# The first head's loads issued behind the last stores of the first stage, on two queues, and the bound's stores issued by ScalarE

## The chip, the cores and the metric

The kernel runs on one core of one Trainium2 chip. The metric is device time in microseconds of one execution. A core has TensorE (PE, matmuls), VectorE (DVE), ScalarE (ACT), GpSimd (POOL) and SyncE (SP), which run side by side and wait for each other on semaphores, and 16 DMA engines, to which SyncE and ScalarE both issue transfers through queues of their own.

## What is computed

A transformer block on x of shape (4, 2048, 256), in float32: a layer norm, then attention with 16 heads of width 16 and an FFN with weights of plus and minus one, both on the normalised x, and both added to x.

```python
xn = _layernorm(x)
# attention: b=4, n=2048, d=256, H=16, Dh=16
q = _rope(split(xn @ Wq + bq)); k = _rope(split(xn @ Wk + bk)); v = split(xn @ Wv + bv)
scores = jnp.einsum('bhnd,bhmd->bhnm', q, k) / jnp.sqrt(jnp.float32(d))
inter = jnp.einsum('bhnm,bhmd->bhnd', jax.nn.softmax(scores, axis=-1), v)
attn = inter.transpose(0, 2, 1, 3).reshape(b, n, d) @ Wo + bo
# FFN: connection weights k0 (512x1024), k1 (1024x1024), k2 (1024x256) are booleans, read as +1 / -1
h = s0 * conn(k0, concat([xn, -xn])); h = relu(h) * 2
h = s1 * conn(k1, h); h = relu(h) * 2
h = s2 * conn(k2, h)
return x + attn + h
```

## The kernel before

The program has three blocks, one behind the other, each ended by a barrier of all engines. `prepare` is the first stage, `maxima` is left at once on these inputs (a branch on a flag, `loose`), and `attend` takes nearly all of the time.

**prepare** works through the 8192 tokens in NC = 16 chunks of 512, numbered c. For a chunk, ScalarE issues the load of x and normalises it, TensorE turns it (`turn`) and projects it to queries, keys and values, VectorE multiplies by the rotary tables (`products`), GpSimd adds the two products (`turned`, L557) and subtracts the high part (`parts`, L550), and ScalarE makes the square and the high part (`part`, L399 and L402). SyncE stores, each 512 KB: the normalised chunk (`store_x`, L298), four pieces of queries and keys split into high and low parts (`store_parts`, L305; in the trace q_parts and k_parts, two calls each), and the values (L340). All of these go to DRAM. The buffer `parts` has four places, so L402 of one piece waits until the store of the piece four before has landed. In SyncE's program a chunk runs: two stores of key parts (of the chunk before), the normalised chunk c + 1, two stores of query parts, the values. The order is written out by hand in the loop behind `store_x(0)`.

Into this loop other transfers are put by hand. `load_first(c)` issues at c = 5 the loads of two biases, at FIRST_HEAD_AT = 13 two tiny DMAs that write a row of zeros into `q_rows` (`row_of_bound`, L311) and the first half of what attend needs for its first head, at c = 14 the second half and the load of the first 512 tokens (`xT_lo`, L321). Half a head is five DMAs in `load_rows` (L806 to L810): keys 256 KB, keys again 128 KB, and three loads of queries of 64 KB. The data are those of the first batch, stored in chunks 0 to 3. In DRAM the parts are an array of [4, 64 x 8, 2048], so the 32 rows that the first DMA writes come from a view with an outer dimension of 4 (4 x 8 rows), and the 16 rows of each of the others from a view with an outer dimension of 2 (2 x 8 rows). Rows are 8 KB for keys and 4 KB for queries.

Behind chunk 15 a bound on all scores is worked out by a chain over several engines (`keep_norms`, `bound_scores`, the square root on ScalarE at L454, `spread_bound`). VectorE fills `bound_fill` with it and SyncE writes it into the first head's rows (`row_of_bound`, L311) and, for the other heads, into DRAM (`store_shift`, four DMAs of 128 KB, L276). SyncE then waits at L351 to L359 until all loads and stores of the stage but those of `store_shift` have landed, and the block ends. VectorE in the meantime splits `xT_lo` (L702, L704), which waits for its load.

**attend** runs 16 passes of four heads. TensorE's first matmuls of scores (L1029) use head 0, which prepare has loaded. SyncE first waits for `bound_stored`, which counts the landed DMAs of `store_shift`, and then loads head 1 with `load_rows`, now all twelve DMAs (L806 to L812; the last of each half is the bound's row, 8 KB), the values of head 1 and the residual. A head is loaded when the one two before it is done with its scores.

```python
            sp.wait_ge(first_loaded, 16 * (LOADS - 2))
            sp.wait_ge(fill_stored, FILLS)
            sp.wait_ge(bound_row, 32)
```

Of the kernel before, what the change touches and what calls it, by code (L numbers as in the profile page):

```python
# [22 lines left out]
F32 = mybir.dt.float32  # L23
# [5 lines left out]
P = 128  # L29
B, N, D, H = 4, 2048, 256, 16  # L30
DH = D // H
T = B * N
G = B * H
# [8 lines left out]
PARTS = 2  # L42
# [5 lines left out]
FIRST_HEAD_AT = 13  # L48
# [88 lines left out]
def prepare(nc, a, w, scratch, bound_stored):  # L137

    ctx = ExitStack()
    with ctx:  # L140
# [126 lines left out]

        def here(c):
            return slice((c % CB) * C, (c % CB + 1) * C)

        @block.sync
        def _(sp):
            def store_shift(a, filled, landed):
                to = scratch["shift"][a].rearrange("g (h w n) -> w (g h) n", h=P // G, n=FILL)
                for n in range(G * N // (P * FILL)):
                    sp.dma_start(to[n], filled.bitcast(F32)).then_inc(landed, 16)  # L276

# [15 lines left out]
            store_shift(1, fill[:], fill_stored)  # L293
# [64 lines left out]
        def _(act):  # L358
# [93 lines left out]
            part(4 * NC - 1)  # L452
# [885 lines left out]
```

## Time and profile before

| | |
|---|---|
| time, median of 3 runs | 2648.11 us (2647.49 to 2648.26) |
| the profiled execution: its own time | 2645.93 us |
| the profiled execution: its span | 2644.1 us |
| TensorE busy | 2577.4 us, 97% of the span |
| ScalarE busy | 2099.3 us, 79% |
| VectorE busy | 977.5 us, 37% |
| GpSimd busy | 300.0 us, 11% |
| first stage (prepare) | from 0 to about 240 us |
| mean granted clock of TensorE | 0.989 of full speed |

The span runs from the first instruction to the last of the profiled execution; its own time has some 2 us more around it. Busy time is the time in which an engine computes; issuing a DMA or waiting does not count. In the view by stretches a row gives, for a piece of the span, the busy time of each engine in us with the number of instructions in brackets (PE, PEld for weight loads, DVE, ACT, POOL), the clock granted to TensorE as a part of full speed, the mean busy share of the 16 DMA engines (packets that overlap on one engine can bring it above 1), and what they moved in GB/s.

### The profile page before, as it was taken

The numbers are of one execution on the slowest core, as the hardware profiler recorded it, in microseconds if no ns is written. First come the engines' busy times: TensorE is split into PE (matmuls) and PEld (weight loads), VectorE is DVE, ScalarE is ACT, GpSimd is POOL, SyncE is SP. The second block draws the span as 40 slices with busy tenths as digits, with TensorE's granted clock in tenths as the row PEclk, the third lists the DMA queues.
The fourth block names the chain that finished last, engine by engine and source line by source line (L and its number), as shares of the span: only waits on it lengthen the run. The fifth ranks groups of instructions, "written<-read, shape, count | busy, mean of one in ns | idle before, by whom it ended". The sixth has DMA issues, their size and how long they took to land.

```text
span 2644.1 us, 49178 instructions
## 1 busy us (share of the span) xinstructions
PE 2577.4 (97%) x20711; PEld 1340.4 (51%) x20711; DVE 977.5 (37%) x1665; ACT 2099.3 (79%) x2342; POOL 300.0 (11%) x268
## 2 busy tenths in 40 slices
PE   7886999999999999999999999999999999999999
PEld 5663454444445454545445454544445454544545
DVE  7773323343324233243324233243324233242323
ACT  6885888888888878788887878788887878788884
POOL 6783000000000000000000000000000000000000
PEclk9997999999999999999999999999999999999999
DMA  9995111111212112121212212121212212121212
GB/s 283 294 292 171 37 47 52 53 61 49 57 43 75 51 48 71 50 77 53 78 44 70 63 46 70 53 77 51 77 43 67 61 53 69 57 77 49 77 38 97
DMA packets 202199, 210.45 MB, mean 80 GB/s; under 512 B 144685, under 2 KB 148605, under 8 KB 195577
## 3 DMA queue, kind: packets, MB, share of 16 engines
q1 hardware_dynamic: 199672, 198.91, 25.1%
q10 hardware_dynamic: 2304, 8.39, 0.9%
q8 instruction: 163, 2.67, 0.4%
q14 instruction: 60, 0.48, 0.1%
HBM read 131.34 MB, written 75.89 MB: 78 GB/s over the span
## 4 chain that ended last, share of the span: by engine, by line
PE 91%; ACT 0%; DVE 0%; issue 0%; DVEq 0%; SPq 0%
PE ps_o L1042 37%; PE ps_f L1075 27%; PE ps_s L1029 24%; PE ps_y L1088 2%; PE ps_s L1124 0%; PE ps_f L1124 0%; ACT probs L1009 0%; DVE probs L1266 0%; PE ps_f L1132 0%; PE ps_o L1124 0%; PE ps_y L1124 0%; PE ps_s L1132 0%; DVEq L819 0%; PE ps_o L1132 0%; PE ps_y L1132 0%
## 5 line engine op out<-in xcount | busy, mean ns | idle before, releaser
L1009 ACT ACTIVATE probs<-ps_s 128x1024 f32<-128x1024 f32 x2048 | 1930.0, 1034 | 453.1 <-PE ps_s L1029 450.7
L1042 PE MATMUL ps_o<-probs,v_ones 128*32 128x512 f32 x8192 | 1011.3, 600 | 0.0
L1029 PE MATMUL ps_s<-q_rows,k_rows 50*128 50x512 f32 x4096 | 868.9, 439 | 5.1 <-SPq L981 4.1
L1029 PEld LDWEIGHTS ps_s<-q_rows,k_rows 50*128 50x128 f32 x4096 | 365.7, 184 | 672.2 <-ACT probs L1009 600.3
L1042 PEld LDWEIGHTS ps_o<-probs,v_ones 128*32 128x32 f32 x8192 | 200.6, 108 | 418.3 <-issue 295.8
L1075 PE MATMUL ps_f<-h_hi,ffn_w 64*128 64x512 f32 x2048 | 410.2, 393 | 0.0
L1075 PE MATMUL ps_f<-h_lo,ffn_w 64*128 64x512 f32 x2048 | 409.3, 391 | 0.0
L1209 DVE COPY raw<-ps_f 128x512 f32<-128x512 f32 x256 | 164.9, 686 | 560.4 <-PE ps_f L1075 560.4
L1164 POOL TENSOR_TENSOR heads<-heads,sums 128x512 f32<-128x512 f32 x64 | 82.3, 1285 | 2149.8 <-DVE sums L1185 2149.8
L1185 DVE RECIPROCAL sums<-sums 128x128 f32<-128x128 f32 x256 | 226.6, 924 | 1.7
L1075 PEld LDWEIGHTS ps_f<-h_lo,ffn_w 64*128 64x128 f32 x2048 | 198.7, 186 | 34.2
L1075 PEld LDWEIGHTS ps_f<-h_hi,ffn_w 64*128 64x128 f32 x2048 | 197.7, 186 | 23.9
L1176 DVE COPY heads<-ps_o 128x512 f32<-128x512 f32 x64 | 44.3, 692 | 407.8 <-PE ps_o L1042 407.8
L1220 DVE SCALAR_TENSOR_TENSOR h_lo<-raw,h_hi 128x512 fp32r<-128x512 f32 x256 | 177.3, 693 | 8.7
L1075 PE MATMUL ps_f<-ffn_w,h_hi 64*128 64x256 f32 x1024 | 129.0, 277 | 0.0
L1075 PE MATMUL ps_f<-ffn_w,h_lo 64*128 64x256 f32 x1024 | 128.5, 276 | 0.0
L1203 DVE SCALAR_TENSOR_TENSOR rest_sum<-ps_f,ffn_scale,rest_sum 128x512 f32<-128x512 f32 x32 | 22.6, 746 | 246.4 <-PE ps_f L1075 246.4
L1075 PE MATMUL ps_f<-xT_hi,ffn_w 64*128 64x512 f32 x512 | 109.0, 421 | 0.0
L1218 DVE TENSOR_SCALAR h_hi<-raw 128x512 fp32r<-128x512 f32 x256 | 107.3, 419 | 0.0
L1075 PE MATMUL ps_f<-xT_lo,ffn_w 64*128 64x512 f32 x512 | 102.4, 395 | 0.0
L1075 PEld LDWEIGHTS ps_f<-ffn_w,h_lo 64*128 64x128 f32 x1024 | 97.5, 185 | 5.5
L1075 PEld LDWEIGHTS ps_f<-ffn_w,h_hi 64*128 64x128 f32 x1024 | 97.5, 185 | 2.6
(118 smaller groups left out, 1384.6 us busy)
## 6 DMA issues: line engine op xcount, KB each, us to landing
k_rows<-k_parts SPq DMA_DIRECT2D x128, 256.0 KB
q_rows<-q_parts SPq DMA_DIRECT2D x384, 64.0 KB
q_parts<-parts SPq DMA_DIRECT2D x32, 512.0 KB, 8.7
k_parts<-parts SPq DMA_DIRECT2D x32, 512.0 KB, 8.3
k_rows<-k_parts SPq DMA_DIRECT2D x128, 128.0 KB
x_chunk<-in_x ACTq DMA_DIRECT2D x16, 512.0 KB, 7.3
xn_d<-xn_t SPq DMA_DIRECT2D x16, 512.0 KB, 8.6
v_heads<-v_sb SPq DMA_DIRECT2D x16, 512.0 KB, 7.7
```

Of the source, the lines that this page charges most:

```text
L1009: nc.scalar.activation(probs[:, s % PBUF, half * 2 * C:(half + 1) * 2 * C], ps_s[:, half].rearrange("p c n -> p (c n)"), ACT.Exp, scale=SC ...
L1029: last = nc.tensor.matmul(ps_s[:, half, w], k_rows[rows, u, t * P:(t + 1) * P], q_rows[rows, u, half], start=True, stop=True)
L1042: last = nc.tensor.matmul(ps_o[32 * c:32 * c + 2 * DH], v_ones[:, u, t], probs[:, s % PBUF, c * C:(c + 1) * C], start=(t == 0), stop=(t == ...
L1075: last = nc.tensor.matmul(to, lhs, rhs, start=first and stage == 0, stop=final and stage == 1)
L1088: last = nc.tensor.matmul(ps_y[:, n], headsT[:, k, t * P:(t + 1) * P], wo[:, k], start=(k == 0), stop=(k == DT - 1))
L1164: nc.gpsimd.tensor_tensor(heads[:, u], heads[:, u], sums[:, u], ALU.mult).then_inc(heads_ready, 1)
L1176: nc.vector.tensor_copy(heads[:, u], ps_o[:]).then_inc(raw_ready, 1)
L1185: nc.vector.reciprocal(at, at).then_inc(sums_inverted, 1)
L1203: nc.vector.scalar_tensor_tensor(out=to, in0=ps_f[:, bank], scalar=w["scale"][:, 0:1], in1=to, op0=ALU.mult, op1=ALU.add).then_inc(group_u ...
L1209: nc.vector.tensor_copy(raw[:, bank], ps_f[:, bank]).then_inc(group_used, 1)
L1218: nc.vector.tensor_scalar(hi, raw[:, bank], 0.0, None, ALU.max).then_inc(high_ready, 1)
L1220: nc.vector.scalar_tensor_tensor(out=lo, in0=raw[:, bank], scalar=0.0, in1=hi.bitcast(F32), op0=ALU.max, op1=ALU.subtract).then_inc(part_r ...
```

## The change

- The loads of the first head leave chunks 13 and 14. All of them, with the load of `xT_lo`, are issued behind the last two stores of parts: `xT_lo` and the four loads of keys by SyncE (`load_first_keys`), the six loads of queries by ScalarE (`load_queries`), ahead of its square root for the bound.
- The four stores of the bound (`store_shift`) are issued by ScalarE, behind the square root and a table load for Exp, when the bound is filled in. SyncE keeps the two small `row_of_bound`.
- The loads of `bv` and `bo` move from chunk 5 to chunk 4, the two rows of zeros from chunk 13 to chunk 4, all behind the load of `Wo` (`load_constants`).
- `load_rows` is cut into `load_keys`, `load_queries` and `load_shift`. In attend a head is still loaded by the same twelve DMAs, now all keys first, then all queries, then the bound's rows.
- SyncE still waits for all ten loads of the first head at the end of prepare.

```diff
-            def load_first(c):
-                if c == FIRST_HEAD_AT:
-                    sp.wait_ge(k_rows_set, 1)
-                    for w_half in range(2):
-                        row_of_bound(1, fill[:], w_half, zero_row)
-                if FIRST_HEAD_AT <= c < FIRST_HEAD_AT + 2:
-                    load_rows(sp, scratch, 0, w["q_rows"][:, 0], w["k_rows"][:, 0], first_loaded, only=c - FIRST_HEAD_AT)
-                if c == FIRST_HEAD_AT + 1:
-                    sp.dma_start(w["xT_lo"][:].bitcast(F32).rearrange("p k n -> p (k n)"), scratch["xn"][0]).then_inc(first_x_loaded, 16)
-                if c == FFN_WEIGHTS_AT + 1:
-                    sp.dma_start(bv[:], a["bv"].rearrange("(k p) -> p k", p=P), allow_slow_non_contiguous=True).then_inc(bias_loaded, 16)
-                    sp.dma_start(bo[:], a["bo"].rearrange("(o n) -> o n", o=1).broadcast_to([P, D])).then_inc(bias_loaded, 16)
+            def load_constants():
+                sp.wait_ge(w_split, 1)
+                sp.dma_start(w["wo"][:], a["Wo"].rearrange("(k p) n -> p k n", p=P)).then_inc(wo_loaded, 16)
+                sp.dma_start(bv[:], a["bv"].rearrange("(k p) -> p k", p=P), allow_slow_non_contiguous=True).then_inc(bias_loaded, 16)
+                sp.dma_start(bo[:], a["bo"].rearrange("(o n) -> o n", o=1).broadcast_to([P, D])).then_inc(bias_loaded, 16)
+                for w_half in range(2):
+                    row_of_bound(1, fill[:], w_half, zero_row)
+
+            def load_first_keys():
+                sp.dma_start(w["xT_lo"][:].bitcast(F32).rearrange("p k n -> p (k n)"), scratch["xn"][0]).then_inc(first_x_loaded, 16)
+                sp.wait_ge(k_rows_set, 1)
+                load_keys(sp, scratch, 0, w["k_rows"][:, 0], first_loaded)
 
             store_x(0)
             for c in range(NC):
-                load_first(c)
                 if c == FFN_WEIGHTS_AT:
-                    sp.wait_ge(w_split, 1)
-                    sp.dma_start(w["wo"][:], a["Wo"].rearrange("(k p) n -> p k n", p=P)).then_inc(wo_loaded, 16)
+                    load_constants()
...
             store_parts(4 * NC - 2)
             store_parts(4 * NC - 1)
+            load_first_keys()
             sp.wait_ge(fill_ready, 2)
             for w_half in range(2):
                 row_of_bound(0, bound_fill, w_half, bound_row)
-            store_shift(0, bound_fill, bound_stored)
-
             sp.wait_ge(first_loaded, 16 * (LOADS - 2))
...
             part(4 * NC - 1)
+            load_queries(act, scratch, 0, w["q_rows"][:, 0], first_loaded)
             act.wait_ge(bound2_ready, 1)
             nc.scalar.activation(bound[:], bound2[:], ACT.Sqrt).then_inc(bound_ready, 1)
             nc.scalar.activation(std[:, 0, 0:1], eps[:], ACT.Exp)
+            act.wait_ge(fill_ready, 2)
+            store_shift(act, 0, bound_fill, bound_stored)
...
+def load_keys(queue, scratch, g, k_rows, loaded):
+
+    k_head, q_head = heads_of(scratch)
+    for w in range(2):
+        at = GROUP_ROWS * w
+        queue.dma_start(k_rows[at:at + 2 * DH, :].bitcast(F32), k_head[g]).then_inc(loaded, 16)
+        queue.dma_start(k_rows[at + 2 * DH:at + AUG, :].bitcast(F32), k_head[g, 0:2]).then_inc(loaded, 16)
+
+
+def load_queries(queue, scratch, g, q_rows, loaded):
+
+    k_head, q_head = heads_of(scratch)
     q_flat = q_rows.rearrange("p h n -> p (h n)")
     for w in range(2):
         at = GROUP_ROWS * w
         here = slice(w * N // 2, (w + 1) * N // 2)
...
+        queue.dma_start(q_flat[at:at + DH].bitcast(F32), q_head[g, 0:2, :, here]).then_inc(loaded, 16)
+        queue.dma_start(q_flat[at + DH:at + 2 * DH].bitcast(F32), q_head[g, 0:2, :, here]).then_inc(loaded, 16)
+        queue.dma_start(q_flat[at + 2 * DH:at + AUG].bitcast(F32), q_head[g, 2:4, :, here]).then_inc(loaded, 16)
```

SyncE's queue from the values of chunk 12 to the last stores of key parts, before (128x... are the stores of a chunk, 32x, 16x the loads of a head):

```order
L340 DMA v_heads<-v_sb 128x1024
L311 DMA q_rows<-fill 1x4x256 x2
L806 DMA k_rows<-k_parts 32x1x2048
L807 DMA k_rows<-k_parts 16x1x2048
L808 DMA q_rows<-q_parts 16x1x1024
L809 DMA q_rows<-q_parts 16x1x1024
L810 DMA q_rows<-q_parts 16x1x1024
L305 DMA k_parts<-parts 128x2x512 x2
L298 DMA xn_d<-xn_t 128x1024
L305 DMA q_parts<-parts 128x2x512 x2
```

The same again, with the load of `xT_lo` at its end, stands behind the values of chunk 13. After the change the stores of chunks 12 to 15 follow each other with nothing between them, and the keys stand behind the last pair; the end of SyncE's queue in prepare is now:

```order
L304 DMA q_parts<-parts 128x2x512 x2
L337 DMA v_heads<-v_sb 128x1024
L304 DMA k_parts<-parts 128x2x512 x2
L321 DMA xT_lo<-xn_d 128x1024
L801 DMA k_rows<-k_parts 32x1x2048
L802 DMA k_rows<-k_parts 16x1x2048
L801 DMA k_rows<-k_parts 32x1x2048
L802 DMA k_rows<-k_parts 16x1x2048
L310 DMA q_rows<-q_rows 1x4x256 x2
```

Here the four stores of row_shift, which stood behind L311 before, are gone. On ScalarE the end of prepare is, after the change (before, the activations and the table load stood alone):

```order
L812 DMA q_rows<-q_parts 16x1x1024
L813 DMA q_rows<-q_parts 16x1x1024
L814 DMA q_rows<-q_parts 16x1x1024
L812 DMA q_rows<-q_parts 16x1x1024
L813 DMA q_rows<-q_parts 16x1x1024
L814 DMA q_rows<-q_parts 16x1x1024
L451 ACTIVATE bound<-bound 1x1
L452 ACT_TABLE_LOAD
L452 ACTIVATE std<-eps 128x1
L270 DMA row_shift<-q_rows 128x256 x4
```

So six loads of queries come ahead of the square root, and the stores of the bound have moved behind it from SyncE's queue.

## Rows read from the trace of the kernel before

**Rows 1.** the page: busy time and instructions of TensorE; the chain that ended last

```profile
PE 2577.4 (97%) x20711; PEld 1340.4 (51%) x20711; DVE 977.5 (37%) x1665; ACT 2099.3 (79%) x2342; POOL 300.0 (11%) x268
...
PE 91%; ACT 0%; DVE 0%; issue 0%; DVEq 0%; SPq 0%
```

**Rows 2.** chain of waits in order of time, start us, us, what: where attend begins

```profile
240.83 0.81 PE ps_s L1029 x2
```

**Rows 3.** timeline of SyncE's queue, chunks 12 to attend: start us, us, line, DMA

```profile
173.82 2.87 SPq L305 DMA_DIRECT2D k_parts<-parts  x2
...
183.34 2.05 SPq L311 DMA_DIRECT2D q_rows<-fill  x2
185.43 0.70 SPq L806 DMA_DIRECT2D k_rows<-k_parts  x1
...
189.04 1.08 SPq L305 DMA_DIRECT2D k_parts<-parts  x2
...
202.39 2.84 SPq L305 DMA_DIRECT2D k_parts<-parts  x2
...
219.90 2.85 SPq L305 DMA_DIRECT2D k_parts<-parts  x2
...
229.72 1.67 SPq L305 DMA_DIRECT2D k_parts<-parts  x2
234.33 1.29 SPq L311 DMA_DIRECT2D q_rows<-q_rows  x2
235.66 1.90 SPq L276 DMA_DIRECT2D row_shift<-q_rows  x4
240.70 0.76 SPq L806 DMA_DIRECT2D k_rows<-k_parts  x1
```

**Rows 4.** timeline of ScalarE: its two long waits in chunks 13 to 15

```profile
200.39 0.63 ACT L402 ACTIVATE parts<-turned 128x512 fp32r<-128x512 f32 x1 [6.76 <-DMA k_parts<-parts]
...
217.91 0.63 ACT L402 ACTIVATE parts<-turned 128x512 fp32r<-128x512 f32 x1 [8.71 <-DMA k_parts<-parts]
```

**Rows 5.** stretches: busy time by engine (instructions), clock, DMA share, GB/s; first stage

```profile
162.33:173.82 11.49, 10.56 (x61) 8.27 (x61) 9.13 (x21) 11.00 (x20) 10.12 (x9) 1.00 1.05 326
187.00:190.00 3.00, 1.36 (x11) 1.36 (x12) 1.86 (x3) 3.00 (x6) 3.00 (x3) 1.00 0.30 92
...
217.00:220.00 3.00, 0.00 (x0) 0.00 (x0) 0.00 (x0) 2.00 (x4) 1.39 (x2) 0.84 0.15 60
```

**Rows 6.** stretches in attend: head 1 loading, then no load, then head 2 loading

```profile
244.00:249.00 5.00, 4.79 (x22) 3.31 (x22) 0.00 (x0) 3.63 (x5) 0.00 (x0) 0.50 0.24 92
...
254.00:258.00 4.00, 4.00 (x37) 2.06 (x34) 1.55 (x3) 4.00 (x5) 0.00 (x0) 1.00 0.12 51
269.00:278.00 9.00, 9.00 (x76) 4.05 (x70) 2.58 (x5) 6.90 (x8) 0.00 (x0) 1.00 0.00 0
...
293.00:297.00 4.00, 4.00 (x34) 2.02 (x36) 3.91 (x7) 2.96 (x4) 0.00 (x0) 1.00 0.13 52
```

**Rows 7.** a stretch: chunk 15, from its first store of keys to the last

```profile
219.90:229.72 9.82, 4.44 (x20) 2.91 (x20) 3.40 (x5) 5.47 (x10) 9.79 (x8) 0.50 0.70 227
```

**Rows 8.** timeline of SyncE's queue, the load of Wo in chunk 4

```profile
69.53 0.75 SPq L331 DMA_DIRECT2D wo<-in_Wo  x1
71.33 3.08 SPq L305 DMA_DIRECT2D k_parts<-parts  x2
```

**Rows 9.** stretches behind the last stores of parts

```profile
229.70:235.50 5.80, 2.27 (x9) 1.30 (x6) 3.82 (x12) 1.69 (x3) 3.00 (x2) 0.50 1.05 260
235.70:238.20 2.50, 1.06 (x3) 0.34 (x1) 1.15 (x2) 0.00 (x0) 0.00 (x0) 0.50 0.72 210
```

**Rows 10.** SyncE's waits at the end of the first stage

```profile
L355 SPq EVENT_SEMAPHORE  x4: 28/28/333, 237.7 to 238.2; - x4
```

**Rows 11.** timelines of ScalarE and VectorE in the tail

```profile
232.88 0.20 ACT L454 ACTIVATE bound<-bound 1x1 f32<-1x1 f32 x1 [3.23 <-DVE bound L631]
...
235.20 1.23 DVE L704 TENSOR_TENSOR xT_lo<-xT_lo,xT_hi 128x1024 fp32r<-128x1024 f32 x1
```

More of the change, by code:

```diff
@@ L47 @@
 FFN_WEIGHTS_AT = 4
-FIRST_HEAD_AT = 13
 FILL = 256
@@ L266, in prepare, with store_shift @@
         block = ctx.enter_context(nc.Block())
+        def store_shift(queue, a, filled, landed):
+            to = scratch["shift"][a].rearrange("g (h w n) -> w (g h) n", h=P // G, n=FILL)
+            for n in range(G * N // (P * FILL)):
+                queue.dma_start(to[n], filled.bitcast(F32)).then_inc(landed, 16)
         def here(c):
@@ L272, in _ @@
         def _(sp):
[L273 to L276, printed above, removed]
             sp.dma_start(ident[:], a["ident"]).then_inc(ident_loaded, 16)
@@ L292, in _ @@
             sp.wait_ge(zero_ready, 1)
-            store_shift(1, fill[:], fill_stored)
+            store_shift(sp, 1, fill[:], fill_stored)
             def store_x(c):
@@ L794, in heads_of @@
     return (scratch[name].rearrange("am (g e) n -> g am e n", e=HALF) for name in ("k", "q"))
-def load_rows(sp, scratch, g, q_rows, k_rows, loaded, only=None):
+def load_keys(queue, scratch, g, k_rows, loaded):
     k_head, q_head = heads_of(scratch)
-    shift = scratch["shift"].rearrange("a g (w n) -> g w a n", w=2)
+    for w in range(2):
[4 more added lines that the diff above has]
+    k_head, q_head = heads_of(scratch)
     q_flat = q_rows.rearrange("p h n -> p (h n)")
@@ L804, in load_rows, with load_shift @@
         here = slice(w * N // 2, (w + 1) * N // 2)
-        if only in (None, w):
-            sp.dma_start(k_rows[at:at + 2 * DH, :].bitcast(F32), k_head[g]).then_inc(loaded, 16)
-            sp.dma_start(k_rows[at + 2 * DH:at + AUG, :].bitcast(F32), k_head[g, 0:2]).then_inc(loaded, 16)
-            sp.dma_start(q_flat[at:at + DH].bitcast(F32), q_head[g, 0:2, :, here]).then_inc(loaded, 16)
-            sp.dma_start(q_flat[at + DH:at + 2 * DH].bitcast(F32), q_head[g, 0:2, :, here]).then_inc(loaded, 16)
-            sp.dma_start(q_flat[at + 2 * DH:at + AUG].bitcast(F32), q_head[g, 2:4, :, here]).then_inc(loaded, 16)
-        if only is None:
-            sp.dma_start(q_flat[at + AUG:at + ROWS].bitcast(F32), shift[g, w]).then_inc(loaded, 16)
+        queue.dma_start(q_flat[at:at + DH].bitcast(F32), q_head[g, 0:2, :, here]).then_inc(loaded, 16)
+        queue.dma_start(q_flat[at + DH:at + 2 * DH].bitcast(F32), q_head[g, 0:2, :, here]).then_inc(loaded, 16)
+        queue.dma_start(q_flat[at + 2 * DH:at + AUG].bitcast(F32), q_head[g, 2:4, :, here]).then_inc(loaded, 16)
+def load_shift(queue, scratch, g, q_rows, loaded):
+    shift = scratch["shift"].rearrange("a g (w n) -> g w a n", w=2)
+    q_flat = q_rows.rearrange("p h n -> p (h n)")
+    for w in range(2):
+        at = GROUP_ROWS * w + AUG
+        queue.dma_start(q_flat[at:at + PARTS].bitcast(F32), shift[g, w]).then_inc(loaded, 16)
 def attend(nc, a, w, scratch, out, bound_stored):
@@ L895, in load_head @@
             def load_head(g, u):
-                load_rows(sp, scratch, g, q_rows[:, u], k_rows[:, u], rows_loaded[u])
+                load_keys(sp, scratch, g, k_rows[:, u], rows_loaded[u])
+                load_queries(sp, scratch, g, q_rows[:, u], rows_loaded[u])
+                load_shift(sp, scratch, g, q_rows[:, u], rows_loaded[u])
             def load_v(g, u):
```

## The prediction

> **What bounds the kernel now.** The page comes first: TensorE is busy for 97% of the span and holds 91% of the chain that ended last [rows 1]. That is attend, and attend keeps its instructions. So the change can only move the moment at which attend begins, plus whatever its own loads do there. The chain in order of time dates that moment: the first matmul of scores is at 240.83 [rows 2]. Every microsecond by which this comes earlier or later is one in the total.
>
> Next, SyncE's timeline [rows 3], read for the pace of the chunks. Two stores of keys are issued at the start of each. An undisturbed chunk takes 11.49 us from one such issue to the next [rows 5]. From 173.82 on the distances are 15.22, 13.35, 17.51 and 9.82 us. The first three are long, and what stands between them are the two halves of the first head's loads. ScalarE's timeline shows how it hurts: L402 waits 6.76 and 8.71 us for the landing of a store of parts [rows 4].
>
> Third, why a few loads cost so much. The stretches say it. In the undisturbed chunk the DMA engines have a share of 1.05 and move 326 GB/s. From 187 to 190 and from 217 to 220 the share is 0.30 and 0.15, 92 and 60 GB/s [rows 5], while everyone waits for a DMA. A share of 0.15 is 2.4 of 16 engines. So most engines have run empty, and some two still work off a backlog.
>
> Attend shows the same loads without other traffic. With no head on the way the share is 0.00. While head 1 (issued from 240.70 on [rows 3]) and head 2 come in, it is 0.24, that is 4 engines, and then 0.12 and 0.13 at 51 and 52 GB/s, that is **two engines at 25.5 to 26 GB/s each** [rows 6]. I read it with the code: the view with outer dimension 4 goes over four engines, those with outer dimension 2 over two. Of 1152 KB, engines 0 and 1 (my names for the two) then carry per half 256/4 + 128/2 + 3 x 64/2 = 224 KB, in all 448 KB each, or 459 thousand bytes. At 25.5 GB/s that is **18.0 us**, although the whole, spread evenly, would be 72 KB per engine. The rows agree with it: head 1 is issued from 240.70 on, and at 254 to 258 the two engines are still busy.
>
> **Step 1: chunks 13 to 15 without the loads.** Chunk 12 starts its key stores at 173.82. Chunks 12 and 13 then take the undisturbed 11.49 us each. Chunk 14 loads no x any more (3.0 MB in place of 3.5), so it lies between the undisturbed pace, 11.49, and that of GpSimd, which has eight operations per chunk and is busy 9.79 of 9.82 us in chunk 15 [rows 7]; I take 10.3, nearer to GpSimd's, since 11.49 x 3.0/3.5 is 9.85. Chunk 15 stays at GpSimd's 9.82. The last stores of keys are then issued at 173.82 + 2 x 11.49 + 10.3 + 9.82 = 216.9, in place of 229.72: **-12.8 us** (-11.6 with 11.49 for chunk 14, -13.3 with 9.82). The issue of the loads (from 185.43 to 189.04 for the first half) goes with them and is part of the distances.
>
> **Step 2: the end of the stage.** Call the issue of the last key stores T (229.72 before, 216.9 now). Before, SyncE passed its last wait at 238.2 [rows 10], T + 8.5. Its waits were nearly all over by then: what set the end was the chain of the bound, two small DMAs and 1.90 us for four stores of row_shift [rows 3]. Now, behind T, engines 0 and 1 have to do in turn:
> - the stores that are under way or just issued: until T + 5.8, the stretch with a share of 1.05 in the rows of before [rows 9];
> - `xT_lo`, 512 KB over 16 engines, 33 thousand bytes each at 25.5: 1.3 us;
> - the loads of the first head: 18.0 us;
> - the stores of row_shift, 512 KB at 210 GB/s in the stretch in which they ran before [rows 9]: 2.5 us, of which I count 1.6, since ScalarE's queue shares the engine with SyncE's and small packets leave room.
>
> Sum T + 26.7, with a half microsecond for the last landing and the wait T + 27.2, that is 244.1 in place of 238.2. So step 2 costs **+18.7 us**. That the loads come from two queues changes nothing in it: the engines are the bottleneck, not the issue. Two queues save issue time only, at most 10 x 0.70 us, and this lies far inside the 27 us.
>
> The bounds. Below: engines 0 and 1 take the stores of the tail faster, since the total is what limited them there (260 GB/s is 16 per engine), by the bytes: values, two stores, `xT_lo`, row_shift are 5 x 33 thousand at 25.5, 6.4 us, with 18.0 and a start of 1.5 gives T + 25.9. Above: while stores run, the engine gives 326/16 = 20.4 GB/s; all 459 thousand bytes at that are 22.5 us, T + 31.7.
>
> The Trainium skill (DMA: Bandwidth & Descriptors, Specifications) states about 27 GiB/s per engine. By that, as an estimate, 459 thousand bytes would take 15.8 us, and the change would cost 2.2 us less than in my sum. The rows show 25.5 to 26, so they decide here.
>
> **Step 3: what is hidden.** ScalarE issues six loads (0.70 us each as SyncE's [rows 3], 4.2) ahead of its square root, which was due at T + 3.2 [rows 11]; the bound comes some 1.0 us later, then SyncE's two small DMAs. All that is done by T + 9, hidden by the loads; with that cover gone it would cost 1.0. VectorE's split of `xT_lo` ran to 236.4 [rows 11]; now it waits for the landing, T + 8 to T + 13, plus 1.23 us and two shorter instructions: hidden, too. SyncE saves the 1.90 us of row_shift, which count for nothing behind the loads. Attend's SyncE waits for `bound_stored` before head 1; those stores are in front of the last keys or level with them, and head 1 has a whole head's time to come in (the two-engine stretches of heads 1 and 2 lie 39 us apart [rows 6]), so nothing waits. The other order of the twelve DMAs in attend is free for that reason. TensorE's clock is at its lower level, 1.2 GHz, at attend's start already (0.50 in the stretch from 244 to 249 [rows 6]), so a longer wait ahead of it has nothing more to take.
>
> **Step 4: the constants.** In chunk 4 SyncE now issues two biases (as Wo, 0.75 each) and two rows of zeros (2.05 [rows 3]) ahead of the key stores at 71.33 [rows 8]. Without them Wo ended 1.05 us before that, so the store goes out some 2.5 us late. The DMA engines have a backlog there as everywhere in these chunks (share 1.05), so its landing moves little: 0, at most +2. In chunk 13 the rows of zeros fell into free time (183.34 to 185.39), so taking them away brings nothing.
>
> **Sum:** -12.8 + 18.7 + 0 = **+5.9 us**. Against the profiled execution's 2645.93 that is 2651.8; this execution lies 2.2 below the median of the runs, 2648.11, so for the median 2654.0. About 0.2% (5.3 us) is what a measurement of this kernel can tell from no change, so the forecast stands just beyond it. Its own range, from the bounds: -13.3 + 17.4 = +4.1 to -11.6 + 23.2 + 1 = +12.6; the upper end needs everything to go wrong together, so 2651.5 to 2658.5.
>
> **Rivals.**
> - *The two queues work on different engines.* No row shows narrow loads from ScalarE, whose only DMAs are the wide loads of x. If its six went to another pair of engines, the keys alone would be 256 KB on SyncE's pair, 10.3 us, and the end T + 5.8 + 1.3 + 10.3 + 1 = T + 18.4, 235.3: -2.9 us, 2645.2, no change that can be told. In attend all loads come from one queue and share one pair, which says nothing on this. The Trainium skill (the same page, "Why a DMA increments its semaphore by 16 and not by 1") says that such a DMA takes the lowest-numbered engines whichever of the two queues it is on, and no run here shows it yet.
> - *The loads hide in the tail (the other side).* If the two-engine plateau were attend's own, and the loads ran wide, 1.7 MB at 326 GB/s are 5.2 us behind T + 5.8, the end T + 11.5 at 228.4: -9.8, 2638.3. It decides at T + 21.3: a load stage that ends before that makes the kernel faster. Against it: in chunks 13 to 15 the same few engines were seen at work [rows 5].
> - *The chunks gain less.* If chunk 14 and 15 find another wait, so that each keeps some 1.9 us of the length that it had, step 1 is worth -9, and the time is 2657.8. For it: chunk 14 of before took 17.51 us, and that the loads made all of this is read off, not shown.
> - *A small loss.* Step 1 is right, but the two engines catch up in the tail more than I grant: +2 to +5, 2650 to 2653.
>
> **How the numbers follow.** Forecast 0.55, queues on different engines 0.10, hidden 0.07, less gain 0.10, small loss 0.18. Slower by over 0.2% (above 2653.4): 0.45 of the forecast's 0.55 and the less gain, 0.55. Within 0.2%: the rest of the forecast, the small loss, most of the different engines: 0.36. Faster: 0.09. The range takes the forecast, the small loss and less gain, and reaches down to half of the first rival: 2646.5 to 2659.
>
> **What would show it.** Right: issues of key stores every 11.5 us up to chunk 14, the last near 217; the waits of L402 on key stores gone; then a stretch of some 15 us with a share of 0.12 to 0.25 at 50 to 100 GB/s, SyncE waiting at the end of prepare for `q_rows` or `k_rows`, and TensorE's first scores near 247. Wrong: a share of 0.25 to the end with 4 engines busy (first rival), or first scores before 240.8.

## The result and the profile after

The changed kernel takes 2653.26 us (median of 20 runs, 2651.21 to 2655.72), the kernel before 2647.60 us in the same series (20 runs, 2645.21 to 2650.29). The ratio is 1.0022 with a 95% interval of 1.0015 to 1.0029: **slower by 5.7 us**, where +5.9 was forecast. The profiled execution of the changed kernel took 2651.77 us with a span of 2650.0, the one of before 2645.93 and 2644.1. Of the runs below, one of the eleven executions of e1 was slow (4905.28 us) and has no part in its ratio.

SyncE's timeline of the changed kernel, from chunk 12 to attend (start us, us, line, DMA):

```profile
173.40 2.85 SPq L304 DMA_DIRECT2D k_parts<-parts  x2
...
184.76 2.86 SPq L304 DMA_DIRECT2D k_parts<-parts  x2
...
194.92 2.88 SPq L304 DMA_DIRECT2D k_parts<-parts  x2
...
205.77 2.97 SPq L304 DMA_DIRECT2D k_parts<-parts  x2
...
216.82 1.66 SPq L304 DMA_DIRECT2D k_parts<-parts  x2
218.52 1.11 SPq L321 DMA_DIRECT2D xT_lo<-xn_d  x1
219.68 0.73 SPq L801 DMA_DIRECT2D k_rows<-k_parts  x1
...
222.48 1.27 SPq L310 DMA_DIRECT2D q_rows<-q_rows  x2
247.33 0.75 SPq L801 DMA_DIRECT2D k_rows<-k_parts  x1
```

The key stores now go out at distances of 11.36, 10.16, 10.85 and 11.05 us, where they were 15.22, 13.35, 17.51 and 9.82 [rows 3]. The last are issued at 216.82 in place of 229.72: 12.9 us have been won in the chunks. Then SyncE issues its loads at once, 0.73 us for a load of keys, and is done with everything at 223.75. But its first DMA in attend is issued at 247.33, where it was 240.70.

ScalarE's six loads do not stand strictly behind the last stores. ScalarE does not wait for SyncE, and its first load goes out 1.2 us ahead of T, the issue of the last key stores (216.82). Its timeline:

```profile
215.60 1.23 ACTq L812 DMA_DIRECT2D q_rows<-q_parts  x1
```

What SyncE did in between is in the view of its own waits (engine line, waited for: us in total, times, longest us), and in the line of that wait:

```profile
SPq L351 <- DMA q_rows<-q_rows: 20.8, 1, 20.8
```

```profile
L351 SPq EVENT_SEMAPHORE  x4: 28/28/18867, 223.9 to 244.8; - x4
```

L351 is the wait for the first head's loads, 20.8 us, over at 244.8. Before, the line that answers to it was passed at 238.2 with next to no wait [rows 10]. The view by stretches of the changed kernel shows for what it waited (busy time by engine, clock, DMA share, GB/s):

```profile
187.00:190.00 3.00, 2.97 (x20) 2.27 (x21) 3.00 (x5) 3.00 (x7) 3.00 (x4) 1.00 1.00 193
205.77:216.82 11.05, 3.63 (x24) 2.10 (x22) 3.40 (x5) 6.21 (x11) 9.90 (x8) 0.88 0.91 274
216.80:222.60 5.80, 1.47 (x7) 0.57 (x3) 2.92 (x10) 1.69 (x3) 3.00 (x2) 0.50 1.05 226
220.00:224.00 4.00, 1.87 (x5) 1.64 (x6) 0.89 (x5) 1.69 (x3) 0.00 (x0) 0.50 1.09 177
228.00:234.00 6.00, 0.00 (x0) 0.00 (x0) 2.25 (x3) 0.00 (x0) 0.00 (x0) 0.50 0.29 111
234.00:244.00 10.00, 0.00 (x0) 0.00 (x0) 0.00 (x0) 0.00 (x0) 0.00 (x0) 0.50 0.13 51
```

The hole of before at 187 to 190 [rows 5] is filled: share 1.00, 193 GB/s. In its place stands the stretch from 234 to 244: no engine computes, and the DMA share is 0.13 at 51 GB/s, as head 1 (0.12 at 51) and head 2 (0.13 at 52) had shown in attend [rows 6]. By the prediction's count these are two engines with 448 KB each, now with the whole core waiting. TensorE's first scores, with the idle time ahead of them in brackets:

```profile
247.46 1.22 PE L1042 MATMUL ps_s<-q_rows,k_rows 50*128 50x512 f32 x4 [22.70 <-SPq L994]
```

247.46 in place of 240.83 [rows 2] is 6.6 us later; the span grew by 5.9. Attend gave back 0.7 us. That fits TensorE's clock: it rises to 2.4 GHz about 7.6 us behind the first scores (at 255.1) where it took about 8.9 before (at 249.8), and 1.3 us less at half the clock are 0.65 us. The stretches of 1 us in which it rises, before and then after:

```profile
249.00:250.00 1.00, 1.00 (x10) 0.38 (x11) 0.23 (x1) 0.94 (x1) 0.00 (x0) 0.62 0.25 87
```

```profile
255.00:256.00 1.00, 1.00 (x10) 0.57 (x6) 0.09 (x1) 0.83 (x2) 0.00 (x0) 0.92 0.13 50
```

### The profile page after: what moved, and what is told of

Read it like the earlier page. It is cut to its first block, busy times and chain, and to the rows that moved or that the text cites. A ratio compares the mean times of both kernels' runs of the same rounds, so it can differ in the third digit from the quotient of the medians.

```text
span 2650.0 us, 49178 instructions
## 1 busy us (share of the span) xinstructions
PE 2572.1 (97%) x20711; PEld 1334.4 (50%) x20711; DVE 978.3 (37%) x1665; ACT 2099.1 (79%) x2342; POOL 299.9 (11%) x268
## 4 chain that ended last, share of the span: by engine, by line
PE 90%; ACT 0%; DVE 0%; issue 0%; DVEq 0%; SPq 0%
PE ps_o L1055 36%; PE ps_f L1088 27%; PE ps_s L1042 24%; PE ps_y L1101 2%; PE ps_s L1137 0%; PE ps_f L1137 0%; ACT probs L1022 0%; DVE probs L1279 0%; PE ps_f L1145 0%; PE ps_o L1137 0%; PE ps_y L1137 0%; PE ps_s L1145 0%; DVEq L830 0%; PE ps_y L1145 0%; PE ps_o L1145 0%
## 5 line engine op out<-in xcount | busy, mean ns | idle before, releaser
L1042 PE MATMUL ps_s<-q_rows,k_rows 50*128 50x512 f32 x4096 | 868.3, 439 | 23.7 <-SPq L994 22.7
```

The lines of the kernel that those rows point to most:

```text
L1042: last = nc.tensor.matmul(ps_s[:, half, w], k_rows[rows, u, t * P:(t + 1) * P], q_rows[rows, u, half], start=True, stop=True)
```

## The experiments

All of e1 to e12 are timed in five rounds against the kernel before. In this table T is the issue of the last key stores in the profiled execution, and the next column the first scores of attend; the last is the median less that of before in the same series. T and the first scores are each from one execution. Runs with the same order of stores in the chunks differ by up to 1.6 us in T (the change and e1 to e4: 215.27 to 216.82), so less than that in T is not read as an effect.

| run | median us | ratio to before (95% interval) | T | first scores | behind T | us against before |
|---|---|---|---|---|---|---|
| before | 2647.60 | 1 | 229.72 | 240.83 | 11.1 | 0 |
| the change | 2653.26 | 1.0022 (1.0015 to 1.0029) | 216.82 | 247.46 | 30.6 | +5.7 |
| e1: change, loads of 8 rows | 2641.91 | 0.9982 (0.9973 to 0.9991) | 216.08 | 236.72 | 20.6 | -4.3 |
| e2: change, queries of 8 rows | 2648.07 | 1.0005 (0.9996 to 1.0015) | 215.27 | 242.04 | 26.8 | +1.9 |
| e3: change, one queue | 2653.58 | 1.0025 (1.0016 to 1.0035) | 216.79 | 248.38 | 31.6 | +7.4 |
| e4: change, bound by SyncE | 2650.86 | 1.0017 (1.0008 to 1.0026) | 216.19 | 246.19 | 30.0 | +4.6 |
| e5: before, loads of 8 rows | 2641.91 | 0.9984 (0.9975 to 0.9993) | 224.12 | 235.40 | 11.3 | -4.3 |
| e6: change, rows together | 2627.06 | 0.9928 (0.9914 to 0.9941) | 205.36 | 222.16 | 16.8 | -19.1 |
| e7: before, rows together | 2623.43 | 0.9914 (0.9901 to 0.9928) | 208.41 | 219.15 | 10.7 | -22.7 |
| e8: e7, chunks 14 and 15 | 2624.64 | 0.9917 (0.9904 to 0.9931) | 209.09 | 219.58 | 10.5 | -21.5 |
| e9: before, bound by ScalarE | 2647.65 | 1.0003 (0.9994 to 1.0012) | 231.03 | 242.57 | 11.5 | +0.8 |
| e10: e7, 8 rows | 2627.73 | 0.9931 (0.9917 to 0.9944) | 211.81 | 222.54 | 10.7 | -19.2 |
| e11: e6, 8 rows | 2628.94 | 0.9934 (0.9920 to 0.9947) | 206.06 | 223.81 | 17.8 | -17.9 |
| e12: e6, two engines | 2720.85 | 1.0283 (1.0269 to 1.0297) | 205.55 | 239.60 | 34.1 | +74.0 |

### e1: the same bytes over more engines

```diff
-        queue.dma_start(k_rows[at:at + 2 * DH, :].bitcast(F32), k_head[g]).then_inc(loaded, 16)
-        queue.dma_start(k_rows[at + 2 * DH:at + AUG, :].bitcast(F32), k_head[g, 0:2]).then_inc(loaded, 16)
+        for m in range(4):
+            queue.dma_start(k_rows[at + HALF * m:at + HALF * (m + 1), :].bitcast(F32), k_head[g, m]).then_inc(loaded, 16)
+        for m in range(2):
+            row = at + 2 * DH + HALF * m
+            queue.dma_start(k_rows[row:row + HALF, :].bitcast(F32), k_head[g, m]).then_inc(loaded, 16)
...
+        for n, m in enumerate((0, 1, 0, 1, 2, 3)):
+            row = at + HALF * n
+            queue.dma_start(q_flat[row:row + HALF].bitcast(F32), q_head[g, m, :, here]).then_inc(loaded, 16)
```

> The changed kernel with the first head's ten loads cut into 24 of 8 rows each (one outer slice of the DRAM view per DMA), the same bytes from the same two queues in the same place. Theory (two DMA engines carry 448 KB each): with outer dimension 8 a DMA goes over 8 engines, the busiest engine carries 144 KB, 5.8 us at 25.5 GB/s in place of 18.0, so 12 us less at the end of prepare: first scores near 235 in place of 247.5, about 2641.5 us, and no stretch with a DMA share of 0.13. Rival 1 (the bytes behind the last stores cost, however spread): no change, 2653. Rival 2 (number of DMAs and their issue cost): 14 more at 0.65 us, 7 per queue, slower than the changed kernel by up to 4 us.

Measured: 2641.91, 4.3 us less than before and 10.0 less against before than the change. The first scores came at 236.72, 20.6 behind T in place of 30.6. A stretch of its profile where the changed kernel had two engines:

```profile
229.00:232.00 3.00, 0.00 (x0) 0.00 (x0) 2.25 (x3) 0.00 (x0) 0.00 (x0) 0.50 0.50 199
...
234.00:236.00 2.00, 0.00 (x0) 0.00 (x0) 0.00 (x0) 0.00 (x0) 0.00 (x0) 0.50 0.00 0
```

Share 0.50 is eight engines, at 199 GB/s 24.9 each, and from 234 on nothing is left. There are more DMAs than in the change and the same bytes in the same place, and the time fell: this is against both rivals named. The time from T to the first scores fell by 10.0, where 12.2 was expected from the two-engine sum. The loads themselves ran at the expected 25 GB/s per engine, so the missing 2 us lie elsewhere behind T; no run shows where.

### e2: half of the dose

```diff
-            load_queries(act, scratch, 0, w["q_rows"][:, 0], first_loaded)
+            first_queries(act, scratch, 0, w["q_rows"][:, 0], first_loaded)
```

(`first_queries` is the loop over six slices of e1; the keys stay as in the change.)

> The changed kernel with ScalarE's six loads of queries cut into twelve of 8 rows, SyncE's keys as they are. A half dose of the first run. Theory: the two engines keep 256 KB of keys each and get 48 KB of queries in place of 192, 304 in place of 448 KB, 144 KB less at 25.5 GB/s: 5.8 us less than the changed kernel, 2647.5, with the stretch of two engines shorter by that. Rival (the queries are not on the engines of the keys, so only the keys set the end): no change, 2653. Rival (what the 8-row cut gained came of the keys' shape alone): no change too.

Measured: 2648.07, +1.9 against before where the change has +5.7: 3.7 us less than the change, where 5.8 were expected. (That the median is so near to the expected 2647.5 is owed to a series in which before, too, took 1.4 us less.) This speaks against the first rival of the prediction as well: the queries are ScalarE's, and making them wide shortens the wait for SyncE's keys by 3.8 us (26.8 behind T in place of 30.6). So **both queues' narrow loads ran on the same two engines**.

### e3 and e4: the two other parts of the change undone

```diff
-            load_queries(act, scratch, 0, w["q_rows"][:, 0], first_loaded)
...
                 load_keys(sp, scratch, 0, w["k_rows"][:, 0], first_loaded)
+                load_queries(sp, scratch, 0, w["q_rows"][:, 0], first_loaded)
```

> The changed kernel with the six loads of queries issued by SyncE behind the keys, so that all ten come from one queue. Theory (both queues' narrow loads run on the same two engines, which are the bottleneck): the same time within 1 us, 2653; SyncE's end of issue moves by 4 us, hidden. Rival (the second queue brings other engines or more rate per engine): slower by 4 to 7 us, 2657 to 2660.

Measured: 2653.58, +7.4 against before where the change has +5.7; the intervals overlap, and the profile has the first scores 1.0 us further behind T. From 234 to 244 its profile reads like that of the change:

```profile
234.00:244.00 10.00, 0.00 (x0) 0.00 (x0) 0.00 (x0) 0.00 (x0) 0.00 (x0) 0.50 0.13 52
```

The second queue is worth 1 to 2 us at the most, and not the 4 to 7 of the rival.

```diff
             for w_half in range(2):
                 row_of_bound(0, bound_fill, w_half, bound_row)
+            store_shift(sp, 0, bound_fill, bound_stored)
...
-            act.wait_ge(fill_ready, 2)
-            store_shift(act, 0, bound_fill, bound_stored)
```

> The changed kernel with the four stores of the bound back on SyncE. Theory: hidden behind the loads, no change (within 1 us of 2653). Rival (ScalarE's issue of them is what gains or costs at the end of prepare): 1.9 us either way.

Measured: 2650.86, +4.6 against before. That is 1.0 us below the change by the differences, with intervals that overlap, and 0.6 us by the place of the first scores behind T. Nothing that five rounds can tell, and in no case 1.9 us.

### e9: the bound's stores by ScalarE, alone, without the cover

```diff
             for w_half in range(2):
                 row_of_bound(0, bound_fill, w_half, bound_row)
-            store_shift(0, bound_fill, bound_stored)
...
             nc.scalar.activation(std[:, 0, 0:1], eps[:], ACT.Exp)
+            act.wait_ge(fill_ready, 2)
+            store_shift(act, 0, bound_fill, bound_stored)
```

> The kernel before with one part of the change alone: the four stores of the bound issued by ScalarE, so nothing of the first head's loads hides it. Rival (my reading in the prediction, that SyncE's 1.90 us of issue for these stores are part of what set the end of prepare): 1.9 us less than before. Theory after a second look: the two small DMAs of the bound's row end their issue at 235.6 and land about 2 us later, and SyncE waited 0.3 us for them at 238.2 even behind the four stores, so no more than 0.5 us is to be had: the same as before.

Measured: 2647.65, ratio 1.0003: no change. The line of SyncE's last waits in this kernel (there L353) is the reason:

```profile
L353 SPq EVENT_SEMAPHORE  x4: 28/28/2707, 237.1 to 239.9; - x4
```

Without the four stores SyncE comes to its wait 1.9 us earlier, at 237.1 behind a T of 231.03, and stands there 2.7 us, until 239.9, for its two small DMAs to land. T + 8.9 in place of T + 8.5. The prediction had said that the issue of these stores was part of what set the end of prepare; it was not.

### e5: the wide loads left among the chunks

The kernel before with the same cut, in `load_first`; nothing else moves.

```diff
                 if FIRST_HEAD_AT <= c < FIRST_HEAD_AT + 2:
-                    load_rows(sp, scratch, 0, w["q_rows"][:, 0], w["k_rows"][:, 0], first_loaded, only=c - FIRST_HEAD_AT)
+                    first_half(sp, scratch, w["q_rows"][:, 0], w["k_rows"][:, 0], first_loaded, c - FIRST_HEAD_AT)
```

> The kernel before, with the first head's loads left in chunks 13 and 14 but cut into 24 DMAs of 8 rows. Theory (the chunks wait for two overloaded engines, 12.8 us for 448 KB each): with 144 KB on 8 engines the excess of chunks 12 to 14 over 11.4 us each falls to about a third, 4 us, so the last key stores go out near 221 and the time is about 2639 (8 to 9 us less than before). Rival (SyncE's issue of the loads holds up the stores behind them): 12 DMAs per half at 0.65 us are 7.8 us in place of 3.6, the stores go out later than before and the time is the same as before or up to 8 us more.

Measured: 2641.91, in the same place as e1. T fell from 229.72 to 224.12, 5.6 us, where 8 to 9 were expected. So of the 12.9 us that the narrow loads cost the chunks, 7 to 8 remain with wide ones. An estimate of what the bytes alone take there is 5.2 us: 1.7 MB at the 326 GB/s of an undisturbed chunk, in which the DMA engines are busy all the time (share 1.05 [rows 5]). SyncE's timeline shows no long hold-up by the issue: the key stores behind the first half go out at 189.39 where they went at 189.04 before. The rival is out, the size of the theory was too large.

### e6 and e7: the rows of a head together in DRAM

```diff
-        "q": dram("q_parts", [2 * PARTS, G * HALF, N], F32),
+        "q": dram("q_parts", [PARTS, G * DH, N], F32),
...
-        q_out = scratch["q"].rearrange("(a m) (b p) (r n) -> b m r p a n", m=2, p=P, n=C)
+        q_out = scratch["q"].rearrange("a (b p m) (r n) -> b m r p a n", m=2, p=P, n=C)
...
-    return (scratch[name].rearrange("am (g e) n -> g am e n", e=HALF) for name in ("k", "q"))
+    return (scratch[name].rearrange("a (g e) n -> g a e n", e=DH) for name in ("k", "q"))
...
+        for n, part in enumerate((0, 1, 0)):
+            queue.dma_start(k_rows[at + DH * n:at + DH * (n + 1), :].bitcast(F32), k_head[g, part]).then_inc(loaded, 16)
...
+        for n, part in enumerate((0, 0, 1)):
+            queue.dma_start(q_flat[at + DH * n:at + DH * (n + 1)].bitcast(F32), q_head[g, part, :, here]).then_inc(loaded, 16)
```

(The same for the keys' array. A store of parts still has 128 rows with two pieces of 2 KB, but the rows of one store now lie 16 KB apart in DRAM in place of 8 KB. In attend the heads are loaded by the new views, too.)

> The changed kernel with another order of rows in DRAM: the 16 rows of a head's high (or low) part lie together, so that each load is one slice of 16 rows (12 loads of the first head in place of 10, same bytes; the stores keep 128 rows of 2 KB pieces). Theory: 16 engines with 72 KB each, 2.9 us in place of the 5.8 of the run with 8 rows: 3 us less than that run's 2641.9, so 2639, first scores near 234. Rival (with the loads spread, something else sets the end of prepare: the bound's chain, the stores of the bound): 2641 to 2642. Rival (the new order makes the stores of parts slower, in all chunks): above 2645.

> The kernel before with the same order of rows in DRAM, loads still in chunks 13 and 14. With 448 KB on the busiest engine chunks 12 to 15 lost 13 us, with 144 KB 8 us; theory: by that slope 72 KB leave some 6.5 us, the time is 2640.5. What stays is the bytes themselves: 1.7 MB at 320 GB/s are 5.3 us in chunks that are limited by the DMA engines. Rival (only the busiest engine matters): 2 us left, 2636.

Measured: 2627.06 and 2623.43, 12 and 17 us below what was expected. The miss is not at the end but in all chunks: T is at 205.36 and 208.41. The stores themselves have become faster. From the DMA issues, the kernel before and e7 (median us from issue to landing in the last column):

```profile
q_parts<-parts SPq DMA_DIRECT2D x32, 512.0 KB, 8.7
k_parts<-parts SPq DMA_DIRECT2D x32, 512.0 KB, 8.3
```

```profile
q_parts<-parts SPq DMA_DIRECT2D x32, 512.0 KB, 4.3
k_parts<-parts SPq DMA_DIRECT2D x32, 512.0 KB, 3.2
```

From 8.7 and 8.3 us to 4.3 and 3.2. The same stretches of the first stage, before and then e7:

```profile
90.00:120.00 30.00, 25.38 (x136) 20.62 (x133) 20.72 (x48) 26.75 (x48) 22.92 (x19) 0.89 0.98 297
120.00:150.00 30.00, 24.50 (x145) 19.50 (x144) 23.28 (x47) 25.28 (x44) 23.06 (x19) 1.00 1.00 301
```

```profile
90.00:120.00 30.00, 26.77 (x155) 21.41 (x154) 23.11 (x49) 28.95 (x50) 26.42 (x22) 1.00 0.89 323
120.00:150.00 30.00, 27.82 (x159) 21.41 (x157) 24.30 (x56) 28.54 (x52) 26.24 (x22) 1.00 0.88 317
```

More bytes at a smaller share (323 GB/s at 0.89 for 297 at 0.98), so the DMA engines are no longer full, and GpSimd is busy 26.4 of 30 us in place of 22.9. This gain has nothing to do with the change under study, which stays a loss on top of it: e6 takes 3.6 us more than e7. No run here says which property of the order makes the gain.

The 2.9 us for the loads did not come true, either. Sixteen engines do not carry them eight times as fast as two. Here is e7 between 178 and 181, where the loads of the first half of the head (issued from 175.59 to 178.34) meet the next stores, against 182 to 188, stores and loads of x.

```profile
178.00:181.00 3.00, 3.00 (x21) 2.21 (x19) 3.00 (x6) 3.00 (x8) 3.00 (x3) 1.00 0.97 124
182.00:188.00 6.00, 5.90 (x36) 4.81 (x34) 2.90 (x5) 4.31 (x8) 5.24 (x5) 1.00 1.05 412
```

In attend of e6 the same loads run with next to nothing beside them (head 1, issued from 222.03 on):

```profile
225.00:228.00 3.00, 2.80 (x12) 1.90 (x14) 0.00 (x0) 2.84 (x3) 0.00 (x0) 0.50 1.04 131
```

All engines are busy at 124 and 131 GB/s, 8 GB/s per engine, where stores run at 412. So these loads wait for something that more engines don't add to; what it is, no run shows. 1.2 MB at 124 GB/s are 9.5 us and not 2.9. The loads of 8 rows in e1 do not have this limit (24.9 GB/s per engine). In e6 the first scores come 16.8 behind T, about what was expected (the 20.6 of e1 less 3), but the stores behind T have become faster as well, so this agreement says nothing for the 2.9 us.

### e8, e10, e11: what is the best place and the best cut

e8 is e7 with `FIRST_HEAD_AT = 14`. e10 and e11 are e7 and e6 with each of the 16-row loads in two of 8 rows:

```diff
-            queue.dma_start(k_rows[at + DH * n:at + DH * (n + 1), :].bitcast(F32), k_head[g, part]).then_inc(loaded, 16)
+            for e in (slice(0, HALF), slice(HALF, DH)):
+                queue.dma_start(k_rows[at + DH * n + e.start:at + DH * n + e.stop, :].bitcast(F32), k_head[g, part, e]).then_inc(loaded, 16)
```

> The run before this one (rows together, loads among the chunks) with FIRST_HEAD_AT = 14, so the halves go out at the start of chunks 14 and 15, which move 3.0 and 2.5 MB of their own in place of 3.5 and 3.0. Theory: these chunks are nearer to GpSimd's pace, 9.8 us, and have DMA time left, so 3 us less than FIRST_HEAD_AT = 13: 2637.5. Rival: the loads land late and hold up the end of prepare, or the last stores: same or 1 to 3 us more, 2641 to 2643.

> Rows together in DRAM and the loads in chunks 13 and 14 (2623.4 with 16-row loads), each load now cut into two of 8 rows, in attend too. The 16-row loads showed a share of 1.0 at only 107 to 143 GB/s, the 8-row loads of the first run 198 GB/s at a share of 0.5. Theory: what the loads cost in the chunks (3 us by the pace of the run without them) is the rate at which they run, so 1 us less, 2622.5. Rival: the number of DMAs on SyncE's queue (24 in place of 12) costs 1 to 3 us, 2625.

> Rows together and the loads behind the last stores on two queues (2627.1 with 16-row loads), each cut into two of 8 rows. Behind the last stores 1.2 MB at 130 GB/s are 9 us, at 198 GB/s 6 us. Theory: 2 to 3 us less, 2624.5, the end of prepare at T + 11. Rival (more issue at the end, 24 DMAs over two queues): same or 1 to 2 us more, 2627 to 2629.

Measured: 2624.64, 2627.73, 2628.94. All three theories missed. The later chunks give nothing (+1.2 against e7). In e10 the twelve loads of a half are on SyncE's queue ahead of the stores, which go out at 181.07 where e7 had 178.38 (0.9 of these 2.7 us are there already when the first load goes out). This fits the rival, the number of DMAs, though the time is 3.6 us above e7 by the differences and it had said 1 to 3. In e11 T is the same as in e6 within 0.7 us and the end is 1.0 further behind it, as its rival said.

### e12: two engines again, in the new order

```diff
-    return (scratch[name].rearrange("a (g e) n -> g a e n", e=DH) for name in ("k", "q"))
+    return (scratch[name].rearrange("a (g e m) n -> g a m e n", e=HALF, m=2) for name in ("k", "q"))
...
-            queue.dma_start(q_flat[at + DH * n:at + DH * (n + 1)].bitcast(F32), q_head[g, part, :, here]).then_inc(loaded, 16)
+            queue.dma_start(q_flat[at + DH * n:at + DH * (n + 1)].bitcast(F32), q_head[g, part, :, :, here]).then_inc(loaded, 16)
```

The same rows go to the same number of partitions, only the outer dimension of the view is 2 in place of 16. (Within a part the order of a head's rows changes, alike for queries and keys.)

> The run with rows together and the loads behind the last stores (2627.1), but each load reads the same 16 rows through a view with outer dimension 2, so that only the number of engines changes, not DRAM's order. This takes the two effects of that run apart. Theory: chunks as fast as there (last key stores near 205), then two engines carry all 1152 KB, 576 KB each, 23 us at 25.5 GB/s: end of prepare near T + 32 in place of T + 13.3, 2645.5, with a stretch at a share of 0.13. Rival (the gain came of DRAM's order, whatever the engines): 2627 to 2630.

Measured for prepare: T at 205.55, as in e6, and the first scores at 239.60, 34.1 behind T in place of 16.8, 17.3 us more, where T + 32 for T + 13.3 had been expected for the end of prepare, 18.7. The stretch in between:

```profile
214.00:236.00 22.00, 0.00 (x0) 0.00 (x0) 2.25 (x3) 0.00 (x0) 0.00 (x0) 0.50 0.14 58
```

That takes the two effects apart: the order of rows is worth 11 us in the chunks, and the outer dimension decides how many engines carry the loads. But the time is 2720.85, 75 us over the theory. The chain that ended last names attend, where every head is loaded in the same way:

```profile
by line: PE ps_o L1052 29.4%; PE ps_f L1085 23.4%; PE ps_s L1039 19.5%; SPq L910 5.9%; SPq L919 2.1%; DMA xT_lo<-xn_d 1.9%; PE ps_y L1098 1.7%; SPq L811 1.6%; SPq L800 1.4%; issue 1.2%; SPq L820 1.2%; DVE raw L1219 0.6%; DVE xT_hi L1200 0.4
```

L910 issues the values of a head and L919 stores one, both on SyncE's queue, and behind them stands the load of the next pass's tokens, `xT_lo`. In one pass of this kernel, of e6 and of the kernel before, SyncE's timeline reads:

```profile
475.77 10.52 SPq L910 DMA_DIRECT2D v_ones<-v_heads  x4
486.33 4.02 SPq L919 DMA_DIRECT2D heads_t<-heads  x4
490.47 0.35 SPq L913 DMA_DIRECT2D xT_lo<-xn_d  x1
```

```profile
448.06 2.05 SPq L910 DMA_DIRECT2D v_ones<-v_heads  x4
450.15 3.77 SPq L919 DMA_DIRECT2D heads_t<-heads  x4
454.04 0.35 SPq L913 DMA_DIRECT2D xT_lo<-xn_d  x1
```

```profile
468.21 9.88 SPq L900 DMA_DIRECT2D v_ones<-v_heads  x4
478.13 4.30 SPq L909 DMA_DIRECT2D heads_t<-heads  x4
482.57 0.35 SPq L903 DMA_DIRECT2D xT_lo<-xn_d  x1
```

Behind narrow loads SyncE needs 10 us to issue four DMAs of 32 KB, behind wide ones 2. From the first load of the head (issued at 463.48, 441.57 and 460.52) to the issue of `xT_lo` it takes 27.0, 12.5 and 22.1 us. The load itself lands 3.4 or 3.5 us after its issue in all three. So it is the issue that comes late, not the load that runs slowly. VectorE stands waiting for `xT_lo`, and behind that wait stands its copy `raw` (L1219), which TensorE needs:

```profile
DVE xT_hi L1200 <- DMA xT_lo<-xn_d: 301.3, 15, 20.9
PE ps_f L1085 <- DVE raw L1219: 39.3, 15, 3.4
```

```profile
DVE xT_hi L1190 <- DMA xT_lo<-xn_d: 231.8, 15, 16.7
```

The last line is that of the kernel before. VectorE's wait alone costs nothing: it is 231.8 us in the kernel before and 76.2 in e6, and both spend 2403 us in attend. In e12 it grows past the slack, and TensorE stands idle once in each of 15 passes, 2.6 us on average. Its granted clock then is at the lower level, 1.2 GHz, for some microseconds:

```profile
494.00:496.00 2.00, 0.00 (x0) 0.00 (x0) 1.97 (x3) 1.07 (x2) 0.00 (x0) 1.00 0.00 0
496.00:498.00 2.00, 1.57 (x7) 1.07 (x9) 1.97 (x5) 0.00 (x0) 0.00 (x0) 0.69 0.00 0
498.00:500.00 2.00, 2.00 (x12) 1.61 (x10) 0.96 (x2) 0.97 (x1) 0.00 (x0) 0.50 0.00 0
```

Over stretches of 2 us through all of attend, TensorE is idle for 41.3 us in e12 and 1.2 in e6, and the busy time lost to the lower clock (one less the granted clock, times the busy time) is 32.6 us against 3.6. Together that is 69 of the 75.6 us by which attend of e12 is longer than that of e6. So the order of SyncE's queue in attend is near an edge that no wait of TensorE in the kernel before shows.

## Why the prediction was right, by its steps

**Reading the two engines.** The plateau of 25.5 GB/s per engine in attend was found again behind the last stores, share 0.13 and 51 GB/s. e1, e2 and e12 changed the number of engines and the bytes per engine. The time from T to the first scores moved by -10.0, -3.8 and (e12 against e6) +17.3 us, where the sums by engine gave -12.2, -5.8 and +18.7. The mechanism is shown, and it came out somewhat smaller each time than the sum.

What the prediction made of it for the chunks was only in part right: it laid their whole loss on the few engines. With the loads spread over eight engines but left in place (e5), 7 to 8 of the 12.9 us stay. For the change this made no difference, since it takes the loads out of the chunks altogether.

**Step 1, -12.8 us.** T was forecast at 216.9 and came at 216.82. By the parts it was less exact: chunk 12 11.36 (11.49), chunk 13 10.16 (11.49), chunk 14 10.85 (10.3), chunk 15 11.05 (9.82). Chunk 13 was faster than the undisturbed pace. The last chunk was not at GpSimd's pace: the DMA engines had a share of 0.91 in it (0.70 before [rows 7]), and L398 (L402 of before) still waited 1.46 and 1.95 us for stores. The sum held because these cancelled, and that it held to 0.1 us is luck.

**Step 2, +18.7 us.** SyncE's last wait was over at 244.8, T + 28.0; T + 27.2 was forecast. The bounds, T + 25.9 and T + 31.7, held it. One reading in this step was wrong: the four stores of row_shift did not set the end of prepare before (e9), though their issue filled the time in which the small DMAs landed. It had no weight in the sum.

**The total.** By the profiled executions, 12.9 us were won up to T and 19.5 lost behind it (T + 28.0 for T + 8.5), and the clock at attend's start gave 0.7 back, which no step had. The steps were right to about 1 us each. That their sum met the measured difference to 0.2 us is luck.

**Step 3, hidden.** VectorE's split waited 9.1 us for `xT_lo` and ended at 233.6, T + 16.8, later than the T + 15 or so of the text and still 11 us inside the loads. ScalarE's square root came at 220.87, T + 4.1, 0.9 later than before, as said. Both are covered. e3 puts the second queue at 1 to 2 us at most, and e4 the bound's stores on ScalarE at nothing that can be told.

**Step 4, the constants.** The key stores of chunk 4 went out at 74.21 in place of 71.33, 2.9 us late, and those of chunk 12 at 173.40 in place of 173.82. Nothing is left of it by then.

**The rivals.** Two pairs of engines: against it e2, and the wait that ended at T + 28.0 and not at T + 18.4. Hidden in the tail: against it the plateau. Less gain in the chunks and a small loss: T and the wait lie within 1 us of the forecast. The small loss (+2 to +5) is not far from the measured +5.7 all the same; it is the place of the wait behind T that speaks against it, not the total.

The Trainium skill's 27 GiB/s per engine (DMA: Bandwidth & Descriptors, Specifications) would have given, as an estimate, +3.7; the plateau stayed at 51 GB/s for two engines, and the result is +5.7. The Trainium skill (DMA: Bandwidth & Descriptors, "Why a DMA increments its semaphore by 16 and not by 1") also says that a DMA issued by SyncE or ScalarE (HWDGE there) which uses k engines takes the lowest-numbered k of the core's 16. e2 agrees in so far as the loads of both queues were on one pair; which numbers these engines have, no run here shows.

## What to carry to other kernels

Moving a transfer out of a busy stage pays only if it fits where it goes: look up how many DMA engines carry it (DMA share times 16 while it runs alone) and set its bytes per engine against the free time there. The loads through views with an outer dimension of 2 or 4 ran here on two or four engines. Cutting them by that dimension was worth 10 us where they had been moved (e1 against the change) and 4 where they had been left (e5 against before).

Moving them paid in none of the layouts tried. Against the same loads left among the chunks it cost 5.7 us with the narrow loads, nothing with 8 rows (e1 and e5), 3.6 with the rows together (e6 and e7) and 1 with both (e11 and e10). The best version of these, e7, takes the kernel before, leaves the loads in chunks 13 and 14 and lays the rows together: 2623.43 us, 0.9914 of before (0.9901 to 0.9928).

## What was not expected of the hardware

- The order of rows in DRAM went with the time of the stores: 512 KB landed after 3.2 to 4.3 us in place of 8.3 to 8.7 with rows 16 KB apart in place of 8 KB, same sizes and same source. Which property does it was not tried.
- Loads of 16 rows into 16 partitions kept all engines busy (share 0.97 and 1.04) at 124 and 131 GB/s, 8 GB/s per engine, while 8-row loads ran at 24.9 per engine with eight engines, 199 GB/s in all. What limits the former (the few partitions written, or the rows read) stays open.
- Loads of heads in attend, hidden in the kernel before, cost some 75 us once their bytes per engine grew from 448 to 576 KB. They did so through the queue: SyncE took 10 us to issue four DMAs of 32 KB behind them, as it had before, and everything that stood behind came later.
